# A cross-attention layer on one core: the first pass with two context buffers, one ScalarE piece per value slot, GpSimd released in the key slots, and a row maximum that does not wait for itself

## The reference: what is computed

```
q = layernorm(x) @ Wq.T + bq ;  k = ctx @ Wk.T + bk ;  v = ctx @ Wv.T + bv
x = x + softmax(q k^T / 4, over 12544 keys) v        (16 heads)
x = x + causal_self_attention(layernorm(x))
x = x + quantised_ffn(layernorm(x))
```

## Time and profile before

| | us |
|---|---|
| median of 3 runs (lowest, highest) | 508.31 (506.67, 509.96) |
| the profiled execution, its own time | 511.06 |
| its span | 509.4 |
| first pass, block 0 to the last fold | until 248.7 |
| second pass | 250 to 450 |
| self-attention and feed-forward | 450 to 509 |

### The profile page before, as it was taken

One profiled execution on the slowest core, in us unless ns is written; L12 is line 12 of the kernel. 1 busy time (PEld: TensorE's weight loads), 2 busy tenths in 40 slices (PEclk: granted clock), 3 DMA queues, 4 the chain that ended last, 5 costly groups with the idle time before them and its releaser, 6 DMA issues.

```text
span 509.4 us, 14309 instructions
## 1 busy us (share of the span) xinstructions
PE 480.5 (94%) x5647; PEld 378.2 (74%) x5647; DVE 290.6 (57%) x424; ACT 377.4 (74%) x416; POOL 102.2 (20%) x101
## 2 busy tenths in 40 slices
PE   6999799999999999996799999999999999989897
PEld 3966677776777676773498899998999988959444
DVE  5669599999999999999669400000000000046575
ACT  4486788888888888876388989989898898925011
POOL 4595322233322233405000000000000000000000
PEclk9999799999999999997999999999999999998799
DMA  8765677766687656986948788877777778000000
GB/s 276 279 237 148 250 285 272 276 225 226 246 309 269 266 213 234 381 335 236 402 166 284 281 309 311 297 258 264 265 266 272 267 285 313 3 2 1 0 0 14
DMA packets 34759, 117.47 MB, mean 231 GB/s; under 512 B 4400, under 2 KB 10416, under 8 KB 34736
## 3 DMA queue, kind: packets, MB, share of 16 engines
q1 hardware_dynamic: 30560, 110.58, 57.7%
q0 software_dynamic: 4032, 6.42, 4.4%
q10 hardware_dynamic: 144, 0.13, 0.1%
HBM read 74.44 MB, written 39.47 MB: 224 GB/s over the span
## 4 chain that ended last, share of the span: by engine, by line
PE 53%; DVE 27%; issue 10%; POOL 4%; ACT 3%; DMA 2%; DVEq 1%; SPq 0%; POOLq 0%; ACTq 0%
PE ps_a L967 20%; PE ps_k L981 18%; DVE block_max L636 13%; DVE early L639 7%; PE ps_k L823 3%; DMA early<-in_ctx 2%; PE ps_a L832 2%; DVE k_lo L603 2%; POOL k_stack L353 2%; ACT early L451 1%; PE ps_a L866 1%; PE ps_a L877 1%; POOL q_stack L381 1%; PE ps_a L1053 1%; DVE early L664 1%
## 5 line engine op out<-in xcount | busy, mean ns | idle before, releaser
L636 DVE TENSOR_REDUCE block_max<-ps_a 128x2 f32<-128x896 f32 x112 | 120.8, 1080 | 1.4 <-PE ps_a L866 1.2
L967 PE MATMUL ps_a<-q_stack,k_stack 128*128 128x256 f32 x784 | 110.1, 292 | 1.4 <-ACT middle L508 1.4
L967 PEld LDWEIGHTS ps_a<-q_stack,k_stack 128*128 128x128 f32 x784 | 98.3, 188 | 13.5 <-issue 11.6
L451 ACT CAST early<-ps_a 128x896 bf16<-128x896 f32 x104 | 94.0, 904 | 8.1 <-PE ps_a L866 8.0
L508 ACT ACTIVATE middle<-ps_a 128x1536 f32<-128x1536 f32 (+1 forms) x56 | 90.2, 1663 | 10.6 <-PE ps_a L967 10.6
L508 ACT ACTIVATE early<-ps_a 128x1536 f32<-128x1536 f32 (+1 forms) x56 | 90.2, 1663 | 7.9 <-PE ps_a L967 7.9
L699 DVE COPY early<-ps_k 128x256 f32<-128x256 f32 x2 | 0.8, 420 | 164.2 <-PE ps_k L981 164.2
L353 POOL TENSOR_TENSOR k_stack<-early,k_stack 128x448 fp32r<-128x448 f32 x52 | 60.2, 1162 | 120.1 <-DVE early L639 107.6
L832 PE MATMUL ps_a<-w_hi,k_stack 128*128 128x256 f32 x392 | 69.4, 300 | 0.0
L639 DVE TENSOR_TENSOR early<-early 128x896 bf16<-128x896 bf16 x104 | 67.3, 647 | 2.9 <-ACT early L451 2.9
L866 PE MATMUL ps_a<-k_hi,q_pair 32*128 32x448 f32 x448 | 54.7, 477 | 11.7 <-ACT early L451 11.0
(11 more groups left out here) (173 smaller groups left out, 427.7 us busy)
## 6 DMA issues: line engine op xcount, KB each, us to landing
k_stack<-k_hi_scratch SPq DMA_DIRECT2D x56, 448.0 KB, 6.1
v_scratch<-early SPq DMA_DIRECT2D x14, 952.0 KB, 6.3
v_in<-v_scratch SPq DMA_DIRECT2D x14, 952.0 KB, 7.8
early<-in_ctx SPq DMA_DIRECT2D x14, 896.0 KB, 5.6
k_hi_scratch<-k_hi SPq DMA_DIRECT2D x28, 448.0 KB, 3.1
k_lo_scratch<-k_lo SPq DMA_DIRECT2D x28, 448.0 KB, 3.6
k_stack<-k_lo_scratch SPq DMA_DIRECT2D x28, 448.0 KB, 6.3
mask_b<-in_maskn POOLq DMA_DIRECT2D x14, 224.0 KB, 5.7
```

Source lines behind the costliest of these rows:

```text
L451: nc.scalar.copy(staged[:, u % 2], pair_scores(u, 0)).then_inc(max_copied, 1)
L636: nc.vector.tensor_reduce(block_max[:, par, 2 * u:2 * u + 2], pair_scores(u, 1), AX.X, ALU.max).then_inc(max_taken, 1)
L967: last = nc.tensor.matmul(ps_a[:, bank, (k % 2) * 2 * Q:(k % 2 + 1) * 2 * Q], k_stack[:, b_par, a, t * P:(t + 1) * P], q_stack[:, a, :, :] ...
```

## The change

- A second context buffer `ctx_b`; block s uses buffer s mod 2, each with a semaphore of its own. The load of block s+2 moves to the front of SP's iteration s and waits for the subtractions of block s, not of block s+1.
- ACT copies one high piece per value slot: in slots 2, 6, 10 of block s pieces 1, 2, 3 of block s+1, and in slot 14 piece 0 of block s+2. This holds from block 0 (slot 14) and block 1 on; the one copy of 1792 columns stays only for block 1.
- POOL's subtraction n waits for a count that moves by two groups per piece: pieces 0 to 3 of block s+1 are released after DVE's updates in slots 14 (of block s-1), 2, 6, 10, each followed by a key slot.
- The fold of the block's maxima has its waits ahead of it and none behind; the last block is not folded. The last steps are one halving more, a reduction of 28 instead of 56, and one negated reduction over the four columns (two parities, `row_max`, `run_max`) of `block_max`, now laid out 16 x 4.

```
-            sp.wait_ge(ctx_split, PIECES)
-            sp.wait_ge(low_context, 1)
             sp.wait_ge(mask_all_in, 16)
-            sp.dma_start(ctx_t, ctx_d[1]).then_inc(ctx_in, 16)
+            sp.dma_start(ctx_bufs[1], ctx_d[1]).then_inc(ctx_in[1], 16)
...
+            sp.wait_ge(low_context, 1)
-            def load(s):
-                sp.wait_ge(ctx_split, s * PIECES)
-                sp.dma_start(ctx_t, ctx_d[s]).then_inc(ctx_in, 16)
+            def load(s, par):
+                sp.wait_ge(ctx_split, (s - 1) * PIECES)
+                sp.dma_start(ctx_bufs[par], ctx_d[s]).then_inc(ctx_in[par], 16)
...
                     s = i * 2 - 2 + par
+                    load(s + 2, par)
                     store_keys(s, par, 0)
-                    load(s + 2)
                     store_keys(s, par, 1)
                     store_values(s, par)
...  (POOL, split_context)
-                        pool.wait_ge(run_taken, (s - 2) * NG + LAG + n + 1)
+                        pool.wait_ge(run_taken, (s - 2) * NG + LAG + 2 * n)
...  (ACT, evacuate)
-                    if not first and not last and slot < 2 * PIECES:
-                        if slot == 0:
+                    if not first and ahead > 0 and slot in (2, 6, 10):
+                        if slot == 2:
                             act.wait_ge(v_projected, s * NV)
-                        high_piece(s + 1, 1 - par, slot // 2)
+                        high_piece(s + 1, 1 - par, slot // 4 + 1)
+                    if ahead > 1 and slot == 14:
+                        act.wait_ge(v_projected, s * NV + 3)
+                        high_piece(s + 2, par, 0)
...  (DVE, maximum)
-                if not (isinstance(s, int) and s == 0):
+                if not (known and s == 0):
+                    if u % LAG == 0:
+                        dve.wait_ge(run_taken, (s - 1) * NG + LAG + u)
                     dve.wait_ge(max_copied, (s - 1) * NG + u + 1)
...
-                if u == NG - 1:
-                    dve.wait_ge(max_taken, s * NG + NG)
-                    nc.vector.tensor_tensor(row_max[:], row_max[:], block_max[:, par, :], ALU.max).then_inc(row_max_ready, 1)
-                    dve.wait_ge(row_max_ready, s + 1)
-                    dve.wait_ge(run_taken, s * NG + NG)
+            def fold_block_maxima(s, par):
+                dve.wait_ge(max_taken, s * NG + NG)
+                dve.wait_ge(row_max_ready, s + 1)
+                nc.vector.tensor_tensor(row_max, row_max, block_max[:, :, par], ALU.max).then_inc(row_max_ready, 1)
...  (in step, behind maximum)
+                    if u == NG - 1:
+                        fold_block_maxima(s - 1, 1 - par)
...  (the end of the pass)
-            while width >= HK // 8:
+            while width >= HK // 16:
...
-            link(nc.vector.tensor_tensor(row_max[:], row_max[:], run_max[:], ALU.max))
-            nc.vector.tensor_scalar(neg_max[:], row_max[:], -1.0, None, ALU.mult).then_inc(row_max_ready, 1)
+            nc.vector.tensor_reduce(neg_max[:], block_max[:, :, :], AX.X, ALU.max,
+                                    negate=True).then_inc(row_max_ready, 1)
```

More of the change, by code:

```diff
@@ L45 @@
 LAG = NG // 2
[L46 removed]
+PREPARE_SLOT = 5
 WARM_FIRST = 12
@@ L152, in perceiver_layer @@
             sem(n) for n in ("bk_in", "bv_in", "mask_all_in", "attn_w_in", "ffn_w_in"))
-        ctx_in = sem("ctx_in")
+        ctx_in = [sem(f"ctx_in{i}") for i in range(2)]
         mask_in = [sem(f"mask_in{i}") for i in range(2)]
@@ L451, in copy_scores, with evacuate @@
                     nc.scalar.copy(staged[:, u % 2], pair_scores(u, 0)).then_inc(max_copied, 1)
-            def evacuate(s, par, first, last=False):
-                if not first:
+            def evacuate(s, par, first=False, ahead=2):
+                if not (isinstance(s, int) and s < 2):
                     act.wait_ge(max_scored, (s - 1) * NG)
@@ L457, in evacuate @@
                 for slot, work in enumerate(PROJECTIONS):
[L458 to L461, removed]
+                    if first and slot == PREPARE_SLOT:
+                        high_context(1, 1)
                     if slot % 2:
@@ L465, in evacuate @@
                         evacuate_values(s, par, work[1])
-                        if first and par == 0 and work[1] == 0:
+                        if first and work[1] == 0:
                             act.wait_ge(eye_in, 16)
@@ L472, in evacuate @@
                     else:
-                        evacuate_keys(s, par, work[1], work[2], first)
+                        evacuate_keys(s, par, work[1], work[2], isinstance(s, int) and s < 2)
                     of_last, u = scored_in(slot)
-                    if not (of_last and first and par == 0):
+                    if not (of_last and first):
                         copy_scores(s - of_last, u)
-                    if not first and not last and slot < 2 * PIECES:
-                        if slot == 0:
+                    if not first and ahead > 0 and slot in (2, 6, 10):
+                        if slot == 2:
                             act.wait_ge(v_projected, s * NV)
-                        high_piece(s + 1, 1 - par, slot // 2)
-            evacuate(0, 0, True)
-            evacuate(1, 1, True)
+                        high_piece(s + 1, 1 - par, slot // 4 + 1)
+                    if ahead > 1 and slot == 14:
+                        act.wait_ge(v_projected, s * NV + 3)
+                        high_piece(s + 2, par, 0)
+            evacuate(0, 0, first=True)
+            evacuate(1, 1)
             with act.Fori(1, NB // 2 - 1) as i:
-                evacuate(i * 2, 0, False)
-                evacuate(i * 2 + 1, 1, False)
-            evacuate(NB - 2, 0, False)
-            evacuate(NB - 1, 1, False, last=True)
+                evacuate(i * 2, 0)
+                evacuate(i * 2 + 1, 1)
+            evacuate(NB - 2, 0, ahead=1)
+            evacuate(NB - 1, 1, ahead=0)
             for u in range(LAG, NG):
@@ L726, in _ @@
                 scores = ps_a[:, g, :].rearrange("p (h k) -> p h k", h=4)
-                link(nc.vector.tensor_reduce(block_max[:, 0, 4 * g:4 * g + 4], scores, AX.X, ALU.max))
+                link(nc.vector.tensor_reduce(block_max[:, 4 * g:4 * g + 4, 0], scores, AX.X, ALU.max))
                 if g % 2 == 0:
-                    nc.vector.tensor_scalar(block_max[:, 1, 4 * g:4 * g + 4], block_max[:, 0, 4 * g:4 * g + 4],
+                    nc.vector.tensor_scalar(block_max[:, 4 * g:4 * g + 4, 1], block_max[:, 4 * g:4 * g + 4, 0],
                                             -1.0 / D ** 0.5, None, ALU.mult).then_inc(self_shifted, 1)
```

34 lines of the change are left out of this document (19 added, 15 removed).

## The result

On the same chip the kernel before had a median of 509.13 us (506.67 to 511.54, 4 runs) and the changed kernel 501.08 us (499.72 to 503.49, 4 runs). The ratio is 0.9864, with a 95% interval of 0.9819 to 0.9908: between 0.9 and 1.8% faster. The forecast was 498.4 with a range of 496.7 to 503.0. The median fell by 8.05 us, where the sum said 9.95. The profiled execution went from 511.06 us (span 509.4) to 500.90 (span 499.2), where 501.1 was forecast.

The account below looks back on a forecast made before the run. DVE bounds blocks 5 to 12, PE close behind, plus block 2's stall; PE becomes the bound. Gains 8.75 + 0.3 + 0.6 + 0.3 = 9.95 take the median from 508.31 to 498.4 us, range 496.7 to 503.0.

Parts of the forecast that it names:

- The stall: Block 2: ACT and then PE wait for block 3's late context load; the second buffer removes this, gaining 5.7.
- The update beside POOL: DVE's update of `running` during a POOL subtraction costs 0.19 more, twice a block; the new releases remove both.
- The fold's step: Time from the fold's start to DVE's next instruction: 0.37 falls to 0.16 without the waits behind it.
- The end: Close of the pass: 0.6 from DVE entering its last work less far behind PE, 0.3 from the shorter final steps.
- the path of the last subtraction: PE's slot 0 through slot 10's update and POOL's last subtraction to PE's next block: 14.95 against 15.01, just fitting.
- rival B's first case: POOL's last subtraction holds PE: path 15.12, twelve block starts pay 0.11 each, time 499.7; the rival's chance 0.23.
- rival E: Fourth subtraction released one update later: PE starts blocks at 17.08, twelve times 2.07, time 523.2; chance 0.05.
- Rivals B to E: B: last subtraction holds PE, 500.5 (0.23); C: DVE stays bound, 502.8 (0.10); D: stall remains, 504.1 (0.05); E: slower, 523.2 (0.05).
- the sign of B: PE waiting for POOL at a block's slot 0 by more than 0.1 would show this rival, chance 0.23.
- block 1: Gain of 0.3, bounds 0 and 0.6: slot 6's scores win 0.54, but POOL's fourth subtraction now needs slot 10's update.
- 11 x 15.01: Blocks 2 to 12 each run at PE's floor as read from block 4: 165.1 instead of 173.85, gain 8.75.
- everything else is behind the pass and moves with it: Work other than the priced parts shifts with the pass's end and was given no gain or loss.

Follow-up runs that it names:

- Experiment 7: Changed kernel with DVE's two waits on itself put back behind the fold; 503.18 us.
- experiment 4: Changed kernel with every POOL subtraction released one DVE update later; 548.81 us.
- Experiment 5: Changed kernel with PE's first-pass loop in three turns of four blocks instead of six of two; 499.43 us.
- Experiment 3: Changed kernel without POOL's wait for DVE's updates, so subtractions wait for ACT's pieces alone; 504.89 us.
- experiment 6: Changed kernel with POOL's subtractions of block 2 alone not held by DVE's updates; 503.55 us.
- Experiment 11: Kernel before with the second buffer and DVE's maxima part, but POOL's releases and ACT's pieces as before; 502.17 us, ratio 0.9880.

## Why the prediction was right, and where it was off

**Right: what bounds, and the order of the sizes.** The stall was the largest part: 5.7 priced, 5.69 won in block 2 (20.70 to 15.01). The load left at 30.04. The update beside POOL was 0.19 longer and is no more. The fold's step was taken as 0.16 and measured 0.17. PE became the bound, and blocks that end without a turn of the loop take 15.01. The end was priced at 0.9 and fell by 0.87: DVE's last update starts 11.45 behind slot 12 instead of 12.04 (0.59, priced at 0.6), and the pass ends 5.86 behind that update instead of 6.14 (0.28, priced at 0.3).

**Right: the path of the last subtraction**, and how near it lies. The fourth subtraction of block 5 starts 13.69 behind PE's slot 0 (90.23 to 103.92), against 13.72 in the sum, and takes 1.14. POOL's signal to PE is 0.13 (44.89 to 45.02), not 0.09, so the path is 14.96 against a floor of 15.01, as priced at 14.95. Experiment 7 lengthened it by the fold's 0.2 and got blocks of 15.16 to 15.24, which rival B's first case had as 15.12; experiment 4 moved its release and got rival E. Rivals B to E did not come about in blocks 3 to 13. At the start of block 2 the sign of B did appear, a wait of 0.70 for POOL, from another cause (see block 1 below).

**Off: PE's floor.** The step "11 x 15.01" failed, since 15.01 was read from block 4 alone. PE's loop turns after every second block, and the blocks with a turn take 15.2. The kernel before showed it in block 3 (65.94 to 81.17, 15.23) and in the 0.16 of issue at 81.17; the prediction passes over both. Five turns are 0.95, and the blocks without one were 0.01 shorter than priced, which leaves the 0.86 by which blocks 2 to 12 fell short, of 1.39 in the whole pass. Experiment 5 shows it: three turns fewer made these blocks 0.58 shorter, 0.19 each.

**Off: block 1.** I gave it 0.3, by the 0.54 that slot 6's scores would win. They did: PE's slot 12 came 11.50 after slot 0 instead of 12.15. But slot 10's update, which now releases POOL, came at 13.73 instead of 13.79. Between lies slot 8's update, first of the kernel before and then of the kernel after, both beside POOL's run of subtractions:

```profile
41.93 0.62 DVE L639 TENSOR_TENSOR early<-early 128x896 bf16<-128x896 bf16 x1
```

```profile
39.39 3.74 POOL L353 TENSOR_TENSOR k_stack<-early,k_stack 128x448 fp32r<-128x448 f32 x3 [0.36 <-POOL q_stack L381]
...
40.78 1.35 DVE L643 TENSOR_TENSOR early<-early 128x896 bf16<-128x896 bf16 x1
...
43.75 1.14 POOL L353 TENSOR_TENSOR k_stack<-early,k_stack 128x448 fp32r<-128x448 f32 x1 [0.62 <-DVE early L643]
...
45.02 1.07 PE L831 MATMUL ps_k<-k_stack,w_hi 128*128 128x448 f32 x4 [0.70 <-POOL k_stack L353]
```

The update lost 0.73 to a subtraction, all that had been won ahead of it, and PE then waited 0.70 for the held fourth one. In the kernel before it was POOL that lost, its four taking 5.34 instead of 4.6. The term counted waits and left out that two engines read the same memory. Experiment 3, with POOL free, took 15.17 for this block, and experiment 6 showed the other side: unheld, the subtraction can hit an update worse.

**Off: what lies behind DVE at the end.** That "everything else is behind the pass and moves with it" was not so for PE's 24 clock-keeping products. They start behind PE's last scores, whatever DVE does, and were hidden by DVE's tail. With the tail 0.9 shorter they were done 0.04 ahead of DVE's last instruction in the first trace, and held the pass for 0.76 behind it in the next. How much of this is in the medians isn't shown: with 19 products the median was 0.4 lower (501.68 against 502.08), less than the runs scatter.

**The median.** The forecast of 498.4 is 2.7 under the measured 501.08. Of these, 1.4 are the pass (0.86, 0.42 of block 1, and 0.1 in the rest), and 0.8 that the kernel before ran at 509.13 on that chip and not at 508.31. The profiled execution came out at 501.1 minus 0.2, but by luck: 1.3 of its fall is clock behind the second pass. What stays open is the other half microsecond of the median; it is less than the runs scatter.

**Which part was worth what.** The buffer alone won 5.03 of the pass, the maxima alone 1.98, both together 8.17, the whole change 8.56. They are worth 1.2 more together. Of this, 0.77 lies in blocks 2 to 12: 0.49 is what blocks 3 and 4 lose when the buffer comes alone, and 0.26 that the stall is longer when the maxima come alone (20.96). Another 0.6 lies at the end, where the 24 products held PE until 0.8 behind DVE with the maxima alone, and until 0.2 behind it with both. Block 1 takes 0.2 off again (15.75 with both). POOL's releases and ACT's pieces bring at most 0.4 of the pass, and by the changed kernel's second trace nothing. Here the prediction had it too evenly: it counted the fold's waits and POOL's place as joint causes. With the waits gone, the prediction's own terms give DVE 15.19 a block even with POOL on two updates (12.24 + 2.40 + 0.17 + 0.38), already near PE's mean of 15.10. Experiment 11 shows that it is no more than 15.11 (166.20 over eleven blocks), so the sum is 0.08 too long somewhere. What POOL's new place takes away then only gives DVE slack.

## What to carry to other kernels

When a change makes another engine the bound, take that engine's floor over a whole turn of its loop, not from the one block that happened to show it. List what the old bound used to hide, products that only keep the clock among it, and ask of each what it does once the cover shrinks. Where a wait keeps one engine off another's memory accesses, look at each stretch by itself: in the steady blocks it saved some 0.4 us each (15.5 without it against 15.1), and in block 1 it cost 0.5.

## What the runs showed of the hardware

**DVE and POOL on the same memory.** An update (two inputs and its output in SBUF) that starts while POOL subtracts is held nearly until POOL is done. At 42.62 in experiment 6 POOL had until 43.73, and the update ended at 44.21, 0.48 later. At 102.18 in the kernel before POOL had until 102.49, and the update ended at 102.97, again 0.48 later, its usual time being 0.62. So the loss is what POOL has left, less 0.14. The same 0.48 stands at 65.08 in experiment 3 (POOL from 64.49 to 65.64, the update until 66.12). The other way round, POOL's subtraction of 60.24 in experiment 3 found 0.26 left of an update and took 1.26 instead of 1.14. Low key parts and maxima, with one input in PSUM, kept their 0.68 and 1.08. This agrees with the Trainium skill, "SBUF — State Buffer", section "Who interferes with whom", by which the two share one read interface, and the order in which they are issued decides which of them is blocked. The held updates of the earlier trace rows were only a mild case.

**A wait on DVE's own semaphore** behind a 0.18 instruction costs 0.20 to 0.22 (0.37 and 0.39 against 0.17).

**A turn of a loop** on PE costs 0.19 when PE is the bound. Where DVE was the bound it can't be seen: in experiment 3 all blocks from 2 on take 15.50 to 15.53.

**The clock.** In experiment 4 a wait of 2.29 at the start of a block, with PE busy for 16.25 of the block's 18.81, was followed by a granted clock of 0.56 from 125.60 to 129.50, and cost 1.24 in slot 2's value products alone. The wait of 0.70 at the start of block 2 of the changed kernel did not: that block stands at 1.00.

**Signals**, from one engine's end to the next engine's start: DVE to POOL 0.07 to 0.09, POOL to PE 0.13 (44.89 to 45.02 in the changed kernel, 90.57 to 90.70 in experiment 7).
